# A two-layer decoder kernel: the routing stage of its mixture of experts worked in batch pairs, and seven of sixteen pairs of the shared expert moved to the combine stage

## The chip, the core and the metric

The kernel runs on one core of a Trainium2 chip. A core has a matmul engine (TensorE, PE in the rows; PEld is its weight load), VectorE (DVE), ScalarE (ACT), GpSimd (POOL) and SyncE (SP, which here only issues DMAs). They run side by side and wait for each other through semaphores. The metric is the device time of one launch in microseconds (us). The kernel before took 4232.36 us, the median of three runs (4230.83 to 4232.46).

## The reference, cut to what matters

The input x has B = 32 batches of S = 100 rows of D = 256 floats. Six blocks are added to it one after another: causal attention, a cross attention, an attention block with a small mixture of experts, a second attention, a wide cross attention, and last a mixture of NE = 8 experts with a shared expert beside them. Only that last block is touched by the change:

```python
def _L1_ffn_ref(x, shared_w1, shared_w2, experts_w1, experts_w2, gate_w):   # x: layer-normed rows
    x_flat = x.reshape(T, D)                                  # T = 3200 rows
    shared = jnp.einsum('td,dh->th', x_flat, shared_w1.T)     # 256 -> 1024
    shared = jnp.einsum('th,hd->td', jax.nn.silu(shared), shared_w2.T)   # 1024 -> 256
    gate_logits = x_flat @ gate_w.T
    top_k_gates, top_k_idx = jax.lax.top_k(gate_logits, TOP_K)            # 2 of 8
    top_k_gates = jax.nn.softmax(top_k_gates, axis=1)
    ...
    h = jnp.einsum('td,ehd->teh', x_flat, experts_w1)
    expert_out = jnp.einsum('teh,edh->ted', jax.nn.silu(h), experts_w2)
    selected = jnp.einsum('ted,te->td', expert_out, gates)
    return (shared + selected).reshape(B, S, D)
x = x + _L1_ffn_ref(_layernorm(x, axis=-1), ...)
```

## The kernel before, in words

Everything is float32, x stays in on-chip memory from the first stage to the last (`g.x`, 100 partitions by 32 batches by 256), and the stages run one after another, each a block with its own semaphores that all engines enter and leave together. The order inside a stage is written out by hand per engine: each engine has a `run(...)` that is called for every batch or tile, in a loop with a few calls unrolled at either end. In the trace a float32 matmul shows as two MATMULs with two weight loads.

The last block of the reference is three stages.

**Routing stage** (`route_phase`, L2423 to L2666). One batch at a time, 32 times. DVE takes the mean and variance (L80, L84), POOL the inverse root (L89, L91), DVE normalises (`route_y`, L96), PE transposes the 100x256 rows (L102), ACT copies them out of PSUM (`route_yT`, L2543). PE then does, in this order, the gate (L2497), the first layer of the shared expert (`shared_hidden`, L2505: 16 matmuls with a 128x128 block of `w_moe_shared` as weights and the 100 columns of one batch moving), two small matmuls that count the rows ahead of each row (`place`, L2512 and L2513), the second layer of the shared expert for the batch before (`shared_out`, L2520: 8 matmuls with the hidden rows as weights and 256 columns moving), and the transposes of the next batch. ACT applies silu to the hidden rows (L2549). DVE ranks the eight gates (`choose`, L2574 to L2578, with L855 to L865), turns ranks and counts into two slots per row (`place`, L2585 to L2602) and adds the shared expert's output to x (L2607). POOL scatters the normalised rows by these slots to a buffer in device memory (`slots`, L2472, two indirect DMAs per batch). At the end DVE works out the gates' softmax and, for the tiles of the next stage, which expert and which slots each has (L2627 to L2666). At the stage's start SP loads the shared expert's weights (L2457) and then the eight experts' weights, 16 times 1 MB (L2460).

**Tile stage** (`tiles_phase`). The scattered rows lie sorted by expert, in tiles of P = 128 rows; TILES = 58 tiles are worked whatever the routing. Per tile PE does 8 matmuls of 512 columns (L2743), transposes (L2752, L2734) and 8 matmuls of 256 columns in two layers of one expert (L2762).

**Combine stage** (`combine_phase`, L2806 to L2862). Per batch POOL gathers two rows per row back (L2826, two indirect DMAs, eight buffers), DVE multiplies them by the gates and adds them to x (L2835, L2837), SP stores the batch (L2858). PE and ACT do nothing here.

## Time and profile before

| | |
|---|---|
| time, median of three runs | 4232.36 us |
| profiled execution, its own time | 4235.83 us |
| its span in the trace | 4233.9 us |
| PE busy, whole span | 3860.0 us, 91% |
| DVE, ACT, POOL busy, whole span | 2055.6, 1657.3, 1428.3 us |
| routing stage | about 3360 to 3660 us |
| tile stage | about 3662 to 4134 us |
| combine stage | about 4137 us to the end |

The span is what the profiler saw between the first and the last instruction. A busy PE is not a PE at its peak: matmuls overlap, and the records' ends are modelled, so the pace of a run of matmuls is read from start to start. The granted clock (PEclk) is the share of TensorE's full speed that the chip allows; 1.00 is 2.4 GHz and 0.50 is 1.2 GHz.

### The profile page before, as it was taken

What the parts mean: (1) busy time and instruction counts of PE and PEld (TensorE: products, weight loads), DVE (VectorE), ACT (ScalarE), POOL (GpSimd) and SP (SyncE); (2) the same over time, 40 slices, a digit from 0 to 9 for tenths busy, and PEclk for the clock granted to TensorE, in tenths of its full rate; (3) what the DMA queues carried; (4) which work ended last, traced back from release to release, by engine and by line L of the source; (5) the groups of instructions that cost most, each with busy time, mean ns of one, the idle gap of its engine ahead of it and who ended that gap; (6) DMA issues with size and microseconds to landing.
All of it is one profiled execution on the core that took longest, in us unless ns stands there. A gap on an engine that the chain in (4) does not pass through costs nothing. (4 is left out here: it accounts for less than half of the span.)

```text
span 4233.9 us, 71248 instructions
## 1 busy us (share of the span) xinstructions
PE 3860.0 (91%) x25328; PEld 2484.8 (59%) x25329; DVE 2055.6 (49%) x6619; ACT 1657.3 (39%) x3559; POOL 1428.3 (34%) x1985
## 2 busy tenths in 40 slices
PE   6997899988999996888799999999999799899990
PEld 4775555555666653444366666666666588666770
DVE  3554666655777764343355455555555344321113
ACT  3553555554333322666344444444444211122220
POOL 0001433334444432011155555555555433100007
PEclk9999999998999998999899999999999799999995
DMA  9200111100000002000000000000000220011103
GB/s 293 112 0 23 46 34 41 37 1 1 1 0 0 1 1 51 1 1 0 11 12 6 7 12 6 6 12 7 6 12 1 99 105 24 26 34 33 32 30 96
DMA packets 80182, 129.31 MB, mean 31 GB/s; under 512 B 17099, under 2 KB 63600, under 8 KB 77296
## 3 DMA queue, kind: packets, MB, share of 16 engines
q1 hardware_dynamic: 71792, 113.28, 8.7%
q0 software_dynamic: 8192, 13.15, 1.1%
q8 instruction: 153, 2.51, 0.2%
q14 instruction: 45, 0.37, 0.0%
HBM read 78.00 MB, written 48.37 MB: 30 GB/s over the span
## 5 line engine op out<-in xcount | busy, mean ns | idle before, releaser
L2101 POOL TENSOR_SCALAR wide_probs<-wide_probs,wide_inverse 100x361 f32<-100x361 f32 x512 | 606.2, 1196 | 0.1
L2282 ACT ACTIVATE wide_probs<-wide_probs,wide_least 100x361 f32<-100x361 f32 x512 | 300.9, 589 | 629.1 <-DVE wide_least L2348 629.1
L2348 DVE CUSTOM_DVE_ANT_0 wide_probs<-banks,wide_bias 100x361 f32<-100x361 f32 x512 | 251.6, 529 | 124.8 <-issue 124.8
L399 PE MATMUL banks<-w_mix_expert,mix_m_x1T 128*100 128x512 f32 x512 | 258.9, 630 | 17.3 <-DVE mix_m_sum L757 15.8
L1822 ACT ACTIVATE rot_h<-banks,w_rot_b 128x800 f32<-128x800 f32 x256 | 223.6, 926 | 130.4 <-PE banks L1694 128.7
L2157 PE MATMUL banks<-w_wide_v,wide_c 64*120 64x512 f32 (+1 forms) x1152 | 263.5, 590 | 2.5 <-DVE wide_v L2334 1.8
L2151 PE MATMUL banks<-wide_c,w_wide_k 64*128 64x361 f32 x1536 | 255.4, 464 | 3.1 <-DVE wide_kT L2331 2.3
L2099 POOL TENSOR_TENSOR wide_hold_pool<-eps 100x1 f32<-100x1 f32 x256 | 50.7, 198 | 580.6 <-DVE wide_inverse L2354 579.1
L2193 PEld LDWEIGHTS banks<-ident,wide_probs 100*120 100x120 f32 (+1 forms) x1536 | 159.3, 172 | 148.3 <-issue 119.2
L2179 PE MATMUL banks<-wide_kT,wide_qT 64*100 64x361 f32 x1024 | 222.3, 511 | 1.7 <-issue 1.6
L2743 PE MATMUL banks<-moe_w,tiles_xT 128*128 x464 | 211.1, 598 | 0.6 <-DVE tiles_xT L2791 0.6
L2762 PE MATMUL banks<-moe_w,tiles_hT 128*128 x928 | 210.0, 380 | 1.0 <-DVE tiles_hT L2796 1.0
L2193 PE MATMUL banks<-ident,wide_probs 100*120 100x100 f32 (+1 forms) x1536 | 204.6, 270 | 6.8 <-POOL wide_probs L2101 6.8
L2354 DVE RECIPROCAL wide_inverse<-wide_rowsum 100x2 f32<-100x2 f32 x256 | 42.5, 166 | 341.6 <-ACT wide_probs L2282 341.6
L2151 PEld LDWEIGHTS banks<-wide_c,w_wide_k 64*128 64x128 f32 x1536 | 148.9, 187 | 91.9 <-ACT wide_kT L2273 4.5
L2210 PE MATMUL banks<-wide_probsT,wide_v 120*64 120x100 f32 (+1 forms) x3072 | 192.1, 260 | 0.5 <-DVE wide_headsT L2362 0.5
L2762 PEld LDWEIGHTS banks<-moe_w,tiles_hT 128*128 128x128 f32 x928 | 172.1, 190 | 22.4 <-issue 1.7
L757 DVE SCALAR_TENSOR_TENSOR mix_m_sum<-banks,mix_m_coef,mix_m_sum 100x256 f32<-100x256 f32 x256 | 123.6, 483 | 123.1 <-PE banks L399 114.3
L1012 POOL TENSOR_TENSOR cross_kroot<-cross_kclip,neg_half 121x8 f32<-121x8 f32 x64 | 104.2, 1638 | 227.2 <-DVE cross_kclip L1434 227.2
L2157 PEld LDWEIGHTS banks<-w_wide_v,wide_c 64*120 64x120 f32 (+1 forms) x1152 | 108.0, 181 | 120.4 <-issue 92.5
L2824 POOL TENSOR_TENSOR combine_hold<-eps 100x1 f32<-100x1 f32 x32 | 9.1, 285 | 488.6 <-DVE combine_slot_i L2831 487.8
L2210 PEld LDWEIGHTS banks<-wide_probsT,wide_v 120*64 120x64 f32 (+1 forms) x3072 | 141.5, 138 | 33.0 <-issue 1.5
(394 smaller groups left out, 7985.0 us busy)
## 6 DMA issues: line engine op xcount, KB each, us to landing
slots<-zeros SPq DMA_DIRECT2D x59, 512.0 KB, 5.7
moe_w<-in_moe_w SPq DMA_DIRECT2D x16, 1024.0 KB, 25.1
cross_c<-in_ctxT SPq DMA_DIRECT2D x32, 270.8 KB, 4.3
wide_c<-in_ctxT SPq DMA_DIRECT2D x32, 270.8 KB, 4.1
tiles_rows<-slots SPq DMA_DIRECT2D x58, 128.0 KB, 2.0
slots<-tiles_out SPq DMA_DIRECT2D x58, 128.0 KB, 1.7
cross_raw<-in_ctx SPq DMA_DIRECT2D x32, 180.0 KB
out<-x SPq DMA_DIRECT2D x32, 100.0 KB
```

The costliest lines, as they stand in the source:

```text
L399: last = nc.tensor.matmul(expert_bank[0:S, :], u.x1T[:, lane, c, :], w.expert[:, c, k * 2 * D:(k + 1) * 2 * D], start=(c == 0), stop=(c == ...
L1822: nc.scalar.activation(t.h[:, u % 2, m, 2 * half:2 * half + 2, :], pair_banks(i), ACT.Tanh, bias=w.b1[:, m:m + 1]).then_inc(h_done[i], 1)
L2101: last = nc.gpsimd.tensor_scalar(t.probs[:, i % RING, j, :], t.probs[:, i % RING, j, :], t.inverse[:, i % RING, j:j + 1], None, ALU.mult)
L2151: last = nc.tensor.matmul(make_bank(lane)[:, 0:CTX], w.k[rows_of(lane), k, at:at + P], t.c[rows_of(lane), of.buf, k, :], start=(k == 0), s ...
L2157: last = nc.tensor.matmul(make_bank(lane)[0:kw, :], t.c[rows_of(lane), of.buf, k, k0:k0 + kw], w.v[rows_of(lane), k, of.hf * BANK:(of.hf + ...
L2179: last = nc.tensor.matmul(scores(j), t.qT[rows_of(j), here.hf, m, lane, :], t.kT[rows_of(j), here.hf, m, lane, :], start=True, stop=True)
L2193: last = nc.tensor.transpose(turned(j)[0:kw, k * S:(k + 1) * S], t.probs[:, i % RING, j, k0:k0 + kw], g.ident[0:S, 0:S])
L2210: last = nc.tensor.matmul(heads_bank[rows_of(j), :], t.v[0:kw, of.hf, k, lane, at:at + WD], t.probsT[0:kw, i % RING, j, k * S:(k + 1) * S] ...
L2282: last = nc.scalar.activation(t.probs[:, i % RING, j, :], t.probs[:, i % RING, j, :], ACT.Exp, bias=t.least[:, i % RING, j:j + 1], scale=-1.0,
L2348: last = nc.vector.tensor_tensor_reduce(t.probs[:, i % RING, j, :], scores(j), t.bias[:, :], -1.0, LARGEST, ALU.add, ALU.min, t.least[:, i ...
L2743: last = nc.tensor.matmul(hid_bank(lane, half), t.xT[:, lane, c, :], f.w1[:, e, c, half * BANK:(half + 1) * BANK], start=(c == 0), stop=(c ...
L2762: last = nc.tensor.matmul(bank(7)[:, 0:D], t.hT[:, m, :], f.w2[:, e, m, :], start=(m == 0), stop=(m == HM - 1))
```

## The change

It has four parts, all in or for the last block.

1. **Pairs in the routing stage.** Each `run` now works a pair of batches: gates, ranks, counts and slots of both lanes in one instruction each, four scatters per pair, and the first shared layer with 200 columns moving. The rows `route_y` lie in four buffers (`ROW_RING`) where there were two. The running count of the second lane is made on DVE (`counted`) before `place` on PE.
2. **Where the shared expert is worked.** The routing stage does it for nine pairs: the eight even ones, spread over two `run`s each, and the last one after the loop. The seven other odd pairs (`LATER_PAIRS` = 1, 3, ..., 13) are done in the combine stage by PE, ACT and DVE, beside the gathers; mean and inverse root of all odd pairs are kept for that in `moe_meanvar` and `moe_rstd`. The store of these pairs waits for their sum.
3. **57 tiles** where there were 58; that is the most that 6400 rows over 8 experts can need.
4. **Loads and tail.** The shared expert's weights are loaded by SP during the wide cross attention stage, and stay until the end. The tables of the tiles are made ahead of the softmax of the gates, and both beside the last pair's matmuls.

```diff
@@ wide_cross_phase, SP
+            for sem, dst, src in g.loads:
+                sp.dma_start(dst, src).then_inc(sem, 16)
             with sp.Fori(1, PAIRS // 2) as two:
@@
-TILES = 2 * ROWS_ALL // P + NE
+TILES = (2 * ROWS_ALL + (NE - 1) * P) // P
+ROW_RING = 4
+HALF_HID = HM // 2
+LATER_PAIRS = list(range(1, PAIRS - 1, 2))
+SHARED_IN_ROUTE = PAIRS - len(LATER_PAIRS)
+def shared_hidden(nc, g, w, yT, half, ready):
+    for m in range(half * HALF_HID, (half + 1) * HALF_HID):
+        for c in range(DC):
+            last = nc.tensor.matmul(g.psum[:, m // 2, m % 2 * LANES * S:(m % 2 + 1) * LANES * S], w.shared1[:, c, m * P:(m + 1) * P], yT[:, c, :, :].rearrange("p l s -> p (l s)"),
+                                    start=(c == 0), stop=(c == DC - 1))
+    last.then_inc(ready, 1)
...
@@ route_phase, GpSimd
+            def scatter(of):
+                pool.wait_ge(s.slots, of.n)
+                nc.gpsimd.tensor_tensor(u.hold[:, of.buf:of.buf + 1], g.eps[0:S, :], g.eps[0:S, :], ALU.add)
+                for lane in range(LANES):
+                    for k in range(2):
+                        nc.gpsimd.indirect_dma_start(slots[:, :], bass.IndirectOffsetOnAxis(ap=slot_i[:, of.buf, lane, k:k + 1], axis=0), u.y[:, of.buf, lane, :],
+                                                     None).then_inc(scattered[of.buf], 16)
+            def run(before, here, after, third):
+                if third:
+                    roots(third)
+                scatter(here)
@@ route_phase, TensorE
+            def run(before, here, after, third):
+                even = here.par == 0
+                gate(here)
+                if even:
+                    hidden(here, 0)
+                else:
+                    shared_out(before, 0)
+                place(here)
                 if after:
                     turn_rows(after)
+                if even:
+                    hidden(here, 1)
+                else:
+                    shared_out(before, 1)
             turn_rows(FIRST)
-            batches(pe, run)
-            pe.wait_ge(s.added, B - 1)
-            shared_out(LAST)
-            pe.wait_ge(s.slots, B)
-            nc.tensor.matmul(bank(7)[0:S, 0:NE], w.all[:, :], u.running[:, 0, :], start=True, stop=True).then_inc(s.totals_ready, 1)
+            runs(pe, run)
+            pe.wait_ge(s.running, PAIRS + 1)
+            nc.tensor.matmul(totals_out, w.all[:, :], u.running[:, 0, 0, :], start=True, stop=True).then_inc(s.totals_ready, 1)
+            hidden(LAST, 0)
+            hidden(LAST, 1)
+            shared_out(LAST, 0)
+            shared_out(LAST, 1)
@@ route_phase, VectorE
-            dve.wait_ge(s.running, 1)
+            def apply(of):
+                if not of.fixed or of.pair >= ROW_RING:
+                    dve.wait_ge(scattered[of.buf], of.earlier_uses(2 * LANES * 16))
+                for lane in range(LANES):
+                    norm_apply(nc, dve, m1, lane, of.lane_n[lane], u.y[:, of.buf, lane, :], g.x[:, of.b[lane], :], s.y)
+                if of.par == 1:
+                    nc.vector.tensor_copy(f.meanvar[:, of.pair, :, :], m1.meanvar[:, :, :])
+                    nc.vector.tensor_copy(f.rstd[:, of.pair, :], m1.rstd[:, :, 0])
...
+            def run(before, here, after, third):
+                choose(here)
+                if after:
+                    apply(after)
+                if third:
+                    stats(third)
+                place(here)
+                if here.par == 1:
+                    add(before)
@@ combine_phase
+            turn_rows(0)
+            for j in range(LATER):
+                pe.wait_ge(s.yT, j + 1)
+                for half in range(2):
+                    shared_hidden(nc, g, w, t.yT, half, hid_ready[half])
+                if j < LATER - 1:
+                    turn_rows(j + 1)
+                shared_out(j)
...
             for k in range(GATHER):
-                add(k, B - GATHER + k, B - GATHER + k + 1, 32 * ROUNDS)
+                slots_of(k)
+            apply(0)
+            for b in range(B):
+                add(b)
+                j, step = b // PER_PAIR, b % PER_PAIR
+                if step == 0 and j + 1 < LATER:
+                    apply(j + 1)
+                if step == 1 and j > 0:
+                    add_shared(j - 1)
@@ combine_phase, SyncE
+                if b // LANES in LATER_PAIRS:
+                    sp.wait_ge(s.shared, LATER_PAIRS.index(b // LANES) + 1)
+                sp.dma_start(out[b], g.x[:, b, :]).then_inc(stored[b % GATHER], 16)
```

TensorE in the routing stage before, one batch of the loop: the gate, the first shared layer, the two count matmuls, the second shared layer of the batch before, the next batch's transposes (here `x2`, `x16` are repeats of one form; a name ahead of the arrow is written, the others are read).

```order
L2497 MATMUL banks<-w_moe_gate,route_yT 100x8 x2
L2505 MATMUL banks<-route_yT,w_moe_shared 128x100 x16
L2512 MATMUL banks<-route_mask,w_moe_earlier 100x8
L2513 MATMUL banks<-route_running,w_moe_all 100x8
L2520 MATMUL banks<-w_moe_shared,route_hidden 100x256 x8
L2491 REGISTER_ALU
L102 MATMUL banks<-ident,route_y 128x100 x2
```

TensorE there now, two pairs (four batches) of the loop, an even and an odd one:

```order
L2545 MATMUL banks<-w_moe_gate,route_yT 100x8 x4
L2437 MATMUL banks<-route_yT,w_moe_shared 128x200 x8
L2551 MATMUL banks<-route_mask,w_moe_earlier 100x16
L2552 MATMUL banks<-route_running,w_moe_all 100x16
L2538 ISA
L2447 MATMUL banks<-ident,route_y 128x100 x4
L2437 MATMUL banks<-route_yT,w_moe_shared 128x200 x8
...
L2563 MATMUL banks<-w_moe_shared,route_hidden 100x256 x8
L2551 MATMUL banks<-route_mask,w_moe_earlier 100x16
L2552 MATMUL banks<-route_running,w_moe_all 100x16
L2538 ISA
L2447 MATMUL banks<-ident,route_y 128x100 x4
L2563 MATMUL banks<-w_moe_shared,route_hidden 100x256 x8
```

The next pair's transposes stand between the two halves of the shared work, where they were the last thing before the next gate; four batches have one shared first layer of 200 columns where they had four of 100.

VectorE in the combine stage before, one batch of the loop:

```order
L2835 SCALAR_TENSOR_TENSOR x<-combine_got,moe_gate,x 100x256
L2836 REGISTER_ALU
L2837 ISA
L2837 SCALAR_TENSOR_TENSOR x<-combine_got,moe_gate,x 100x256
L2831 ISA
L2831 COPY combine_slot_i<-moe_slot_i 100x2
```

VectorE there now, batches 4 and 5 and the start of 6; `combine_y` are the rows for the shared expert and L2977 is its sum:

```order
L2964 SCALAR_TENSOR_TENSOR x<-combine_got,moe_gate,x 100x256
L2966 SCALAR_TENSOR_TENSOR x<-combine_got,moe_gate,x 100x256
L2951 COPY combine_slot_i<-moe_slot_i 100x2
L2958 TENSOR_SCALAR combine_y<-x,moe_meanvar,moe_rstd 100x256 x2
L2964 SCALAR_TENSOR_TENSOR x<-combine_got,moe_gate,x 100x256
L2966 SCALAR_TENSOR_TENSOR x<-combine_got,moe_gate,x 100x256
L2951 COPY combine_slot_i<-moe_slot_i 100x2
L2977 TENSOR_TENSOR x<-x,banks 100x512
L2964 SCALAR_TENSOR_TENSOR x<-combine_got,moe_gate,x 100x256
```

The sum of a shared pair, which waits for PE, stands in DVE's queue ahead of the rest of the gathered batches.

## Rows read from the trace of the kernel before

**Rows 1.** Busy time by stretch: length, then busy (instructions) per engine, PEclk, DMA.

```profile
3371.00:3392.70 21.70, 18.55 (x101) 17.15 (x101) 7.53 (x45) 4.09 (x8) 6.02 (x9) 0.71 1.02 423
3392.70:3641.00 248.30, 236.38 (x1682) 207.52 (x1682) 122.64 (x696) 38.58 (x87) 89.29 (x146) 1.00 0.14 50
3665.00:4133.00 468.00, 465.85 (x1971) 323.43 (x1970) 89.04 (x173) 103.24 (x174) 0.00 (x0) 0.99 0.10 32
4133.00:4234.00 101.00, 0.12 (x1) 0.00 (x0) 37.13 (x97) 0.00 (x0) 74.39 (x96) 0.52 0.35 99
```

**Rows 2.** Timeline, PE, one routing batch: start, length, engine, line, out<-in, count.

```profile
3606.83 0.52 PE L2497 MATMUL banks<-w_moe_gate,route_yT 128*100 128x8 f32 x4 [0.41 <-ACT route_yT L2543]
3607.20 3.79 PE L2505 MATMUL banks<-route_yT,w_moe_shared 128*128 128x100 f32 x32
3610.83 0.26 PE L2512 MATMUL banks<-route_mask,w_moe_earlier 100*100 100x8 f32 x2
3611.13 3.68 PE L2520 MATMUL banks<-w_moe_shared,route_hidden 128*100 128x256 f32 x16
3614.64 0.34 PE L102 MATMUL banks<-ident,route_y 100*128 100x100 f32 x2
3615.39 0.52 PE L2497 MATMUL banks<-w_moe_gate,route_yT 128*100 128x8 f32 x4 [0.41 <-ACT route_yT L2543]
```

**Rows 3.** Timeline, 200-column matmuls of the wide stage.

```profile
3119.78 2.02 PE L2144 MATMUL banks<-wide_yT,w_wide_q 128*128 128x200 f32 x11
```

**Rows 4.** Timeline, DVE and POOL, the same routing batch.

```profile
3607.38 0.17 DVE L2574 COPY route_gates<-banks 100x8 f32<-100x8 f32 x1
3608.76 0.17 DVE L2577 TENSOR_SCALAR route_mask<-route_rank 100x8 f32<-100x8 f32 x1
3611.38 0.17 DVE L2585 TENSOR_TENSOR route_running<-route_running,route_mask 100x8 f32<-100x8 f32 x1 [2.38 <-PE banks L2513]
3612.76 0.25 POOL L2470 TENSOR_TENSOR route_hold<-eps 100x1 f32<-100x1 f32 x1 [4.37 <-DVE route_slot_i L2596]
3613.07 0.17 DVE L2602 TENSOR_REDUCE route_logits<-route_picked 100x16 f32 x1
...
3614.55 0.98 POOL L2472 DMA_INDIRECT slots<-route_y,route_slot_i  x1 [0.30 <-issue]
```

**Rows 5.** DVE group of one line, 3392.7 to 3641: count, busy, mean ns, idle before.

```profile
L2607 DVE TENSOR_TENSOR x<-x,banks 100x256 f32 x29 | 12.2, 421 | 38.4 <-PE banks L2520 38.4
```

**Rows 6.** Timeline, start of the routing stage.

```profile
3360.82 0.10 POOL L2465 MEMSET route_running<- 100x8 f32 x1 [10.25 <-POOLq L2865]
3368.05 0.43 DVE L80 BATCH_NORM_STATS2 route_ln_stats<-x 100x6 f32<-100x256 f32 x1 [8.63 <-DMA w_moe_shared<-in_moe_shared]
3371.20 0.84 PE L2497 MATMUL banks<-w_moe_gate,route_yT 128*100 128x8 f32 x4 [0.41 <-ACT route_yT L2543]
```

**Rows 7.** Timeline, end of routing and start of tiles.

```profile
3649.58 3.70 PE L2520 MATMUL banks<-w_moe_shared,route_hidden 128*100 128x256 f32 x16 [0.52 <-DVE x L2607]
3659.73 0.17 DVE L2666 CAST moe_tile_expert<-route_tile_expert 1x58 int32<-1x58 f32 x1
3664.52 0.66 PE L2734 MATMUL banks<-ident,tiles_rows 128*128 128x128 f32 x2 [11.14 <-DMA tiles_rows<-slots]
3665.80 5.96 PE L2743 MATMUL banks<-moe_w,tiles_xT 128*128 x8 [0.61 <-DVE tiles_xT L2791]
```

**Rows 8.** Timeline, the same line in two tiles running.

```profile
4096.55 3.60 PE L2743 MATMUL banks<-moe_w,tiles_xT 128*128 x8
4104.53 3.60 PE L2743 MATMUL banks<-moe_w,tiles_xT 128*128 x8
```

**Rows 9.** Timeline, combine stage: its first copies, first and last sums.

```profile
4137.13 0.68 DVE L2831 COPY combine_slot_i<-moe_slot_i 100x2 int32<-100x2 int32 x8 [3.48 <-PEq L2865]
4142.67 0.48 DVE L2835 SCALAR_TENSOR_TENSOR x<-combine_got,moe_gate,x 100x256 f32 x1 [4.86 <-DMA combine_got<-slots,combine_slot_i]
4230.29 0.48 DVE L2835 SCALAR_TENSOR_TENSOR x<-combine_got,moe_gate,x 100x256 f32<-100x256 f32 x1 [1.63 <-DMA combine_got<-slots,combine_slot_i]
```

More of the change, by code:

```diff
@@ L2422, in route_phase, with turn_pair @@
+def turn_pair(nc, g, out, rows):
+    for lane in range(LANES):
+        for c in range(DC):
+            at = (c * LANES + lane) * S
+            last = nc.tensor.transpose(out[:, at:at + S], rows[:, lane, c * P:(c + 1) * P], g.ident[0:S, 0:S])
+    return last
 def route_phase(nc, g, w, f, slots, experts_in):
     with ExitStack() as ctx:
-        s = semaphores(nc, ctx, "route", "running y yT_ready yT gates_ready gates cmp ties behind rank mask chosen prefix_ready "
-                       "placed val sum slot slots picked logits larger below gexp gsum grec hid_ready0 hid_ready1 hid0 hid1 out_ready added totals_ready above tiles "
+        s = semaphores(nc, ctx, "route", "running y yT_ready yT gates_ready gates cmp ties behind rank mask chosen counted prefix_ready "
+                       "placed val sum slot slots equal picked logits larger below gexp gsum grec out_ready added totals_ready above tiles "
@@ L2486, in _ @@
             pe.wait_ge(g.loaded.moe, g.total.moe)
-            pe.wait_ge(s.running, 1)
-            def turn_rows(batch):
-                lane, b, n, pairs = batch
-                pe.wait_ge(s.y, n)
-                turn(nc, g, bank(4), u.y[:, lane, :], DC).then_inc(s.yT_ready, 1)
-            def gate(batch):
-                pe.wait_ge(s.yT, batch[2])
-                for c in range(DC):
-                    last = nc.tensor.matmul(bank(5)[0:S, 0:NE], u.yT[:, c, :], w.gate[:, c, :], start=(c == 0), stop=(c == DC - 1))
-                last.then_inc(s.gates_ready, 1)
@@ L2523, in run, with turn_rows, gate @@
-            def run(before, batch, after):
-                gate(batch)
-                shared_hidden(batch)
-                place(batch)
-                if before:
-                    shared_out(before)
+            def turn_rows(of):
+                pe.wait_ge(s.y, of.lane_n[LANES - 1])
+                turn_pair(nc, g, turned, u.y[:, of.buf, :, :]).then_inc(s.yT_ready, 1)
+            def gate(of):
+                pe.wait_ge(s.yT, of.n)
+                for lane in range(LANES):
+                    for c in range(DC):
+                        last = nc.tensor.matmul(gates_out[:, lane * NE:(lane + 1) * NE], u.yT[:, of.par, c, lane, :], w.gate[:, c, :], start=(c == 0), stop=(c == DC - 1))
+                last.then_inc(s.gates_ready, 1)
@@ new lines, in place, with hidden @@
+            def place(of):
+                pe.wait_ge(s.counted, of.n)
+                nc.tensor.matmul(prefix_out, w.earlier[:, :], u.mask[:, :, :].rearrange("s l e -> s (l e)"), start=True, stop=False)
+                nc.tensor.matmul(prefix_out, w.all[:, :], u.running[:, of.par, :, :].rearrange("s l e -> s (l e)"), start=False, stop=True).then_inc(s.prefix_ready, 1)
+            def hidden(of, half):
+                shared_hidden(nc, g, w, u.yT[:, of.par, :, :, :], half, hid_ready[half])
@@ new lines, in shared_out @@
+            def shared_out(of, lane):
+                if lane == 0 and not (of.fixed and of.pair == 0):
+                    pe.wait_ge(s.added, of.shared - 1 if of.fixed else pe.snap(of.shared - 1))
+                for m in range(HM):
+                    if lane == 0 and m % HALF_HID == 0:
+                        pe.wait_ge(hid[m // HALF_HID], of.shared)
+                    last = nc.tensor.matmul(out_bank[:, lane * D:(lane + 1) * D], u.hidden[:, m, lane, :], w.shared2[:, m, :], start=(m == 0), stop=(m == HM - 1))
+                if lane == LANES - 1:
+                    last.then_inc(s.out_ready, 1)
@@ L2554, in _ @@
             keep_rows(FIRST)
-            batches(act, run)
+            runs(act, run)
+            silu(LAST, 0)
+            silu(LAST, 1)
             act.wait_ge(s.below, 1)
@@ L2617, in run, with add @@
+            def add(of):
+                dve.wait_ge(s.out_ready, of.shared)
+                nc.vector.tensor_tensor(x_pairs[:, of.pair, :], x_pairs[:, of.pair, :], out_bank, ALU.add).then_inc(s.added, 1)
+            def run(before, here, after, third):
+                choose(here)
+                if after:
                     apply(after)
-                if before:
+                if third:
+                    stats(third)
+                place(here)
+                if here.par == 1:
```

337 lines of the change are left out of this document (185 added, 152 removed).

## The prediction

> **What bounds the kernel now.** I read the page first (PE busy 91% of the span), then the busy time by stretch, then the timelines of the three stages that the change touches. The stretches say where PE sets the pace. In the running part of the routing stage PE is busy 236.38 of 248.30 us at a granted clock of 1.00, in the tile stage 465.85 of 468.00 us, and in the combine stage not at all, where POOL is busy 74.39 of 101 us [rows 1]. So two of the stages are PE's, and the third is paced by POOL's gathers, with PE free beside it.
>
> In the routing loop a batch takes 8.56 us from gate to gate (3606.83 to 3615.39) [rows 2]. From start to start: gate 0.37, first shared layer 3.63, counts 0.30, second shared layer 3.51, transposes and what follows 0.75. Of this last part two transposes need about 0.36 (0.34 is the record of both), and some 0.4 is the wait of the next gate for ACT's copy [rows 2].
>
> **What a matmul costs, by shape.** The first shared layer is 32 records of 100 columns at 3.63/32 = 113 ns. Two hundred columns moving against one 128x128 weight load take, in the wide stage, (2.02 - 0.33)/10 = 169 ns from start to start; the 0.33 is my estimate of the last record's own length, in proportion to its columns from the second layer, where 16 records of 219 ns spacing span 3.68, so that the last is 0.39 [rows 2, 3]. A pair's first layer was 64 records, 7.26 us; it becomes 32, 5.41 us. The second layer is the same work, 32 records of 219 ns = 7.02 us a pair [rows 2]. A shared pair is 12.43 us of PE.
>
> **The routing stage after.** Two pairs (an even and an odd run) hold one shared pair: four gates 1.48, two counts 0.60 (the 16 columns in place of 8 I price at nothing, since each record is far above its columns' time), eight transposes 1.44, one shared pair 12.43: 15.95 us, where four batches took 34.25. I add 0.15 per run for hand-overs, so 16.25. Eight such: 130.0. The last pair's shared work after the loop: 12.4. Sum at full clock 142.4.
>
> Is PE still the slowest? DVE: from gate to mask it takes 1.55 us, its placing 1.86 us (3611.38 to 3613.24) [rows 4]. With both lanes in one instruction the small ones grow little: I take 2.2 us for choosing (with the new add to the running count), 2.2 for placing, 0.8 for applying, 1.3 for statistics, 0.7 for the sum in every other run. About 7 us a pair against PE's mean of 8.1. Its bound from above is two batches of today without merging, 2 x 122.64/29 = 8.46 us [rows 1]. POOL: a batch's hold and two scatters take 2.77 us (3612.76 to 3615.53) [rows 4], a pair's some 5.7, and 89.29/29 = 3.08 busy per batch with the roots [rows 1], which with the gaps between scatters is about 7.5 us a pair. It fits under 8.1, with little to spare. The wait inside a run is covered as well: PE's count waits for 2.2 us of choosing and has half a first layer (2.7) or a lane of the second (3.5) ahead of it; the copy of the transposed rows now has the other half ahead of the next gate, so the 0.4 us wait per batch goes. The new wait of `apply` on the scatters is for rows four pairs back, over 20 us earlier. Behind it on DVE stand the placing and the sums, and POOL would wait for these; I price it at nothing.
>
> **Its first batches.** They cost more today: 21.5 us for the first two (3371.20 to 3392.7), 4.4 more than two in the loop, at a mean granted clock of 0.71 [rows 1, 6], PE having idled since the wide stage. The price for the new stage lies between nothing and about 11 (all of the 21.7 us at half clock). The nearest row is the start of the tile stage, where the first tile's first layer took 5.96 against 3.60 [rows 7, 8] and some 3.2 us were lost in all; I take 5, because the first runs also wait through a longer start. The Trainium skill ("TensorE: Matmul & The Clock Gate", Part 1) says that the throttled state is the default and that activity releases it. The routing stage's start bears this out only slowly: with PE busy 18.55 of 21.70 us the clock was still 0.71 in the mean. By the page alone the fuller queue would lose no more than the tile stage does, and the sum would be about 2 us lower.
>
> Gate to the end of the last shared matmul: 142.4 + 5 = 147.4. It was 3371.20 to 3653.28 = 282.1 [rows 6, 7]. **-134.7 us.**
>
> **Ahead of the first gate.** DVE began at 3368.05, after the shared weights had landed, while POOL was in the stage at 3360.82; the gate came 3.15 us after DVE [rows 6]. Now the weights are there. DVE starts at about 3361, and takes two batches through statistics, roots (0.84 each on POOL) and transposes at half clock: about 5.3 us, gate at 3366.3. **-4.9.** The moved loads stand in SP's queue behind the context of the first two pairs of the wide stage and ahead of the third's, which is needed tens of us later; that covers their 2 MB. The experts' 16 MB still have to be in by the tile stage: the DMA engines are full until 3392.7 and then for at most 0.14 x 248 = 35 us more [rows 1], some 67 us in all from the stage's start, and the new stage is over 150 long.
>
> **Behind the last shared matmul.** Today 11.24 us pass until the tile stage's first transposes: 6.6 of softmax and tables on DVE, 4.6 of stage change [rows 7]. Now the tables stand beside the last pair's 12.4 us on PE, and only one sum of 512 columns is left, 0.8 with its hand-over (421 ns for 256 columns [rows 5]). **-5.8.** The cover would be gone only if DVE's 7 us of tables began over 5 us late.
>
> **One tile less.** Tiles follow each other at 7.98 us (4096.55 to 4104.53) [rows 8]. **-8.0.**
>
> **The combine stage.** Before, the first add is at 4142.67 and the 32nd at 4230.29: 2.83 us a batch, POOL's pace; the last add ends about 4231.3 [rows 9]. After: PE has seven shared pairs, 7 x 12.43 + six transposes of pairs at 0.7 = 91.2 us. It can start after the slot copies (0.68), the first pair's rows (0.75), transposes at half clock and their copy: 4140.6. With 3.2 lost to the clock, as at the start of the tiles, it ends at 4235.0, and the sum of pair 13 stands in DVE's queue ahead of batches 30 and 31: 0.7 + 2 x 1.05. End of the adds 4237.8. **+6.5.** So PE takes over the pace here from POOL, by little: DVE waits for PE once per pair, and eight gather buffers (22 us of POOL) stand between. The stores of the last six batches go out together in 3 us; a store's own landing is unchanged, and I price this at nothing, with 1 us as the bound.
>
> **Sum.** -134.7 - 4.9 - 5.8 - 8.0 + 6.5 = -146.9. From the profiled execution's own 4235.83 us that is 4088.9; the median of the runs is 3.5 lower, so 4085.5. **I forecast 4086 us.**
>
> **Rivals.**
> 1. *The hand-overs set the routing pace* (DVE and POOL as calculated are at 7 and 7.5 us of 8.1). For: today 0.4 us a batch is lost between transposes and gate [rows 2], and DVE's upper bound of 8.46 is above PE's mean. Against: the order on PE puts half a layer ahead of each wait. If each run loses 1.0 instead of 0.15, 16 x 0.85 = 13.6 more: 4100. At DVE's bound plus the wait for the shared sum, 9 us a pair, 4101.
> 2. *The clock is kept through the stage changes*, which are shorter (5 us of idle PE, not 11), and the combine stage is close to POOL's pace: 5 + 3.2 + 3.2 less: 4075. Against: 0.71 and 0.52 in the rows of all such stretches [rows 1].
> 3. *PE stays at half clock in the combine stage*: 12.43 becomes about 24.5, so 7 x 12 + 4 = 88 more: 4174. For: the granted clock there is 0.52 today [rows 1]; against: PE idles there, and the tiles reach 3.60 us after one slow tile.
> 4. *Slower than before*: the granted clock is low through both stages, because the new mix of short waits and long runs never fills PE. The 142 + 91 us of PE work would need 233 x (1/c - 1) more, and the gain of 147 is gone at a mean clock c of 0.61; at 0.50 the time is 4319. Against: 1.00 at 95% busy in today's loop [rows 1].
> 5. *The change doesn't shorten the routing stage's loads*: if the third pair's context in the wide stage waited for the 2 MB, that stage grows by at most 5 us: 4091.
>
> **Chances.** The forecast 57%, rival 1 20%, rival 2 11%, rival 5 4%, rival 3 5%, rival 4 2%, and 1% for no change. The forecast's own range is 4078 to 4096. The range for 8 in 10 reaches over rivals 1, 2 and 5 and not to 3 and 4: 4070 to 4114; the upper end takes in hand-overs of 1 us together with the longest slow start. A difference under 0.2% (8.5 us) can't be told from no change here. Faster 0.97, same 0.01, slower 0.02.
>
> **What would show it.** In the profile after: gates of even pairs about 16.2 us apart, PE over 95% busy at 1.00 between them; the 200-column shared matmuls at 169 ns; first gate 5 to 6 us after the last wide sum; a gap of about 5.5 us between the last shared matmul and the first tile; 57 tiles at 7.98; in the combine stage DVE waiting for PE about six times, PE busy 90 us. Wrong would be: POOL without idle time in routing, DVE's count later than PE's half layer, or a granted clock near 0.5 in a stage where PE is busy.

## The result, and the profile after

The changed kernel took 4061.6 us (median of four runs, 4055.7 to 4068.1), the kernel before 4231.6: ratio 0.960, 95% interval 0.958 to 0.962. The forecast was 4086, its range began at 4070; the gain is 170 us where 146 were forecast. The profiled execution took 4068.11 us, the slowest of the four, and stands against 4235.83 before.

| Stretch (us, profile to profile) | before | after | change | forecast |
|---|---|---|---|---|
| start to the end of the last VectorE operation of the wide stage | 3359.42 | 3354.94 | -4.5 | 0 |
| to the first gate | 11.77 | 6.27 | -5.5 | -4.9 |
| first gate to end of last shared product | 282.08 | 136.14 | -145.9 | -134.7 |
| to the first tile's transposes | 11.24 | 5.17 | -6.1 | -5.8 |
| tiles | 468.60 | 461.05 | -7.6 | -8.0 |
| stage change | 4.01 | 3.93 | -0.1 | 0 |
| combine, first slot copy to last sum | 94.16 | 95.50 | +1.3 | +6.5 |
| to the end | 2.58 | 3.29 | +0.7 | 0 |

The stretches of the changed stages, busy time and instructions for PE, weight loads, DVE, ACT and POOL, then granted clock and DMA, answer to [rows 1]:

```profile
3361.20:3378.60 17.40, 17.39 (x96) 15.87 (x97) 10.27 (x56) 3.80 (x5) 9.48 (x19) 0.87 1.01 419
3378.60:3476.70 98.10, 98.10 (x625) 88.60 (x624) 69.88 (x367) 16.62 (x26) 72.27 (x114) 1.00 0.39 142
3502.50:3963.60 461.10, 458.87 (x1938) 317.91 (x1938) 87.49 (x170) 101.49 (x171) 0.00 (x0) 0.99 0.10 32
3967.50:4063.00 95.50, 90.98 (x476) 79.36 (x476) 44.51 (x117) 14.51 (x21) 73.74 (x96) 0.97 0.35 100
```

The first row's mean clock of 0.87 is one stretch at half clock, then full clock to the end; before, there were two. The stretches at half clock, two from the kernel before (inside the first of [rows 1]) and then the one of the changed kernel:

```profile
3371.20:3376.80 5.60, 5.60 (x27) 5.60 (x28) 1.44 (x8) 1.75 (x2) 0.32 (x1) 0.50 1.01 427
3380.20:3387.10 6.90, 6.24 (x29) 5.94 (x30) 2.14 (x12) 0.83 (x2) 3.04 (x4) 0.51 1.01 413
3361.20:3365.80 4.60, 4.59 (x18) 4.60 (x19) 2.85 (x14) 1.25 (x1) 0.86 (x3) 0.50 1.01 424
```

Before, the clock was full between 3376.80 and 3380.20, where PE had 1.51 us of work (it waited 2.13 us for the second batch's rows), and then fell again. Now no wait of PE stands there, and the clock does not fall again.

In the stretch 3378.60:3476.70 PE is busy for all of the 98.10 us at full clock: no hand-over costs anything. PE's timeline of one even and one odd run answers to [rows 2]; it has no wait in brackets on any row:

```profile
3408.99 0.79 PE L2545 MATMUL banks<-w_moe_gate,route_yT 128*100 128x8 f32 x8
3409.64 2.95 PE L2437 MATMUL banks<-route_yT,w_moe_shared 128*128 128x200 f32 x16
3412.43 0.27 PE L2551 MATMUL banks<-route_mask,w_moe_earlier 100*100 100x16 f32 x2
3412.54 0.33 PE L2552 MATMUL banks<-route_running,w_moe_all 100*100 100x16 f32 x2
3412.78 0.56 PE L2447 MATMUL banks<-ident,route_y 100*128 100x100 f32 x4
3413.18 2.90 PE L2437 MATMUL banks<-route_yT,w_moe_shared 128*128 128x200 f32 x16
3415.91 0.79 PE L2545 MATMUL banks<-w_moe_gate,route_yT 128*100 128x8 f32 x8
3416.56 3.68 PE L2563 MATMUL banks<-w_moe_shared,route_hidden 128*100 128x256 f32 x16
...
3424.20 0.79 PE L2545 MATMUL banks<-w_moe_gate,route_yT 128*100 128x8 f32 x8
```

Read from start to start: gates 0.65, half a first layer 2.79 and 2.73, counts 0.35, four transposes 0.40; the two runs take 15.21 us (3408.99 to 3424.20).

The start of routing, [rows 6], and its end, [rows 7]:

```profile
3356.38 0.75 DVE L80 BATCH_NORM_STATS2 route_ln_stats<-x 100x6 f32<-100x256 f32 x2 [1.44 <-PEq L3003]
3361.21 1.00 PE L2545 MATMUL banks<-w_moe_gate,route_yT 128*100 128x8 f32 x5 [0.58 <-ACT route_yT L2595]
...
3490.33 0.17 DVE L2734 CAST moe_tile_expert<-route_tile_expert 1x57 int32<-1x57 f32 x1
3497.39 0.69 DVE L2682 TENSOR_TENSOR x<-x,banks 100x512 f32<-100x512 f32 x1 [3.61 <-PE banks L2563]
3502.52 0.66 PE L2810 MATMUL banks<-ident,tiles_rows 128*128 128x128 f32 x2 [5.17 <-DMA tiles_rows<-slots]
```

VectorE now starts behind the stage change, not behind the weights. The tables are done 7 us before the last shared product; only the sum at 3497.39 and the stage change are left. Two tiles running are 7.98 us apart as in [rows 8].

The combine stage, [rows 9]: one pair on PE, and what VectorE waited for in all of it (total, times, longest):

```profile
4035.30 5.58 PE L2437 MATMUL banks<-combine_yT,w_moe_shared 128*128 128x200 f32 x32
4040.71 0.51 PE L2447 MATMUL banks<-ident,combine_y 100*128 100x100 f32 x4
4041.05 7.07 PE L2921 MATMUL banks<-w_moe_shared,combine_hidden 128*100 128x256 f32 x32
4047.96 5.58 PE L2437 MATMUL banks<-combine_yT,w_moe_shared 128*128 128x200 f32 x32
```

```profile
DVE x L2964 <- DMA combine_got<-slots,combine_slot_i: 34.2, 24, 4.8
DVE x L2977 <- PE banks L2921: 12.7, 4, 5.1
```

PE takes 12.66 us a pair (4035.30 to 4047.96), so seven take 88.6, and VectorE waits for PE four times where I had said about six. The last shared sum waits 5.1 us for PE, and two batches' sums stand behind it, so PE's chain ends the stage; by how little, all_route and last_sum show below. A turn of four transposes costs 0.34 (4040.71 to 4041.05), where I had put 0.7.

### The profile page after: what moved, and what is told of

It is laid out like the page before. It is cut to its first block and busy times, and to the rows that moved or that the text cites. A ratio compares the mean times of both kernels' runs of the same rounds, so it can differ in the third digit from the quotient of the medians.

```text
span 4066.3 us, 69091 instructions
## 1 busy us (share of the span) xinstructions
PE 3810.0 (94%) x24746; PEld 2442.7 (60%) x24747; DVE 2014.0 (50%) x6326; ACT 1649.4 (41%) x3515; POOL 1419.9 (35%) x1969
```

## The experiments

The kernels ran in four series, each on another chip, with the kernel before at 4229.5 to 4233.1 us in all of them. Times of one kernel vary by more than most of the edits cost: the changed kernel's median was 4061.6, 4085.9, 4065.2 and 4071.9 us in its four sets of runs, and the runs of tail_late alone lie 17 us apart (what is known of the reasons is told below). So most verdicts are read from the stage that the edit touches, in one profiled execution each:

| kernel | ratio to before (95%) | first gate to last product | combine |
|---|---|---|---|
| after, first runs | 0.960 (0.958-0.962) | 136.14 | 95.50 |
| after again, series 1 | 0.966 (0.964-0.968) | 136.51 | 118.25 |
| all_route, series 1 | 0.983 (0.982-0.985) | 225.67 | 93.46 |
| turn_twice, series 1 | 0.968 (0.966-0.970) | 142.69 | 122.71 |
| turn_last, series 1 | 0.970 (0.968-0.972) | 152.11 | 123.88 |
| after_b, series 2 | 0.961 (0.959-0.963) | 136.46 | 95.62 |
| one_gather, series 2 | 0.961 (0.958-0.964) | 136.46 | 95.61 |
| last_sum, series 2 | 0.960 (0.958-0.962) | 135.97 | 95.49 |
| loads_back, series 2 | 0.963 (0.961-0.965) | 136.28 | 95.55 |
| ring2, series 3 | 0.973 (0.971-0.975) | 184.92 | 95.61 |
| split_cols, series 3 | 0.968 (0.966-0.970) | 151.37 | 108.90 |
| pool_more, series 3 | 0.961 (0.959-0.963) | 136.13 | 97.08 |
| tail_late, series 3 | 0.963 (0.961-0.965) | 137.50 | 97.00 |
| after_c, series 4 | 0.962 (0.961-0.964) | 136.68 | 95.61 |
| keep_first, series 4 | 0.961 (0.959-0.963) | 136.53 | 94.67 |
| code_shift, series 4 | 0.963 (0.961-0.965) | 136.43 | 100.90 |

**The changed kernel again, three times.**

> The changed kernel once more, nothing edited. If the spread of its first four runs (4055.7 to 4068.1 us) is how this program varies, five more lie in the same band, with a median of 4058 to 4064, and a second profile has the routing stage (first gate to the last shared product) at 136.1 us within 0.5 while its span differs by some microseconds in stages that were not changed. Rival: the 4.5 us by which the last VectorE operation of the wide stage came earlier (3354.46 against 3358.94) belongs to the change; then the second profile has it at 3354.5 within 1 again. If it is chance, it lies anywhere between 3351 and 3360.

> The changed kernel a third time. Its first runs gave 4061.6 us with the combine stage at 95.5 us (first slot copy to last sum); the second series gave 4085.9 with 118.3, the other stages alike within 0.4 us, and with ScalarE and VectorE waiting up to 19.5 us on TensorE's results that its records show as long issued. If that belongs to the chip or the series on which it runs, this run shows one of the two levels again, 95 to 96 or 117 to 124 us, and nothing between; if it varies from run to run, the stage lies between them.

> The changed kernel a fourth time, beside the two others of this series. Two levels have been seen in the combine stage, 95.5 to 97 us (two series) and 118.3 (one series). Again one of the two; which of them tells how often the slow one comes.

Medians 4085.9, 4065.2 and 4071.9, where I had expected 4058 to 4064. The routing stage repeats within 0.6 us. Two things do not. First, the last wide operation ended at 3349.65, 3345.45 and 3363.42 us: the 4.5 us are within what chance does (it does more than the 3351 to 3360 that I had allowed), and the rival falls. Second, the combine stage took 118.25 in series 1 and 95.5 to 95.6 in the others; I call these its long and its short level. Series 1, timeline of PE, ACT and DVE in that stage:

```profile
4013.28 5.58 PE L2437 MATMUL banks<-combine_yT,w_moe_shared 128*128 128x200 f32 x32
4026.88 0.84 ACT L2944 ACTIVATE combine_hidden<-banks 128x800 f32<-128x800 f32 x1 [19.53 <-remote]
4027.86 3.70 PE L2921 MATMUL banks<-w_moe_shared,combine_hidden 128*100 128x256 f32 x8 [7.82 <-ACT combine_hidden L2944]
4032.61 0.84 ACT L2944 ACTIVATE combine_hidden<-banks 128x800 f32<-128x800 f32 x1 [4.89 <-remote]
4034.74 0.74 DVE L2958 TENSOR_SCALAR combine_y<-x,moe_meanvar,moe_rstd 100x256 f32<-100x256 f32 x2 [12.00 <-remote]
```

By its records PE had half of the first layer at 4016.1; ScalarE, which had been free since 4007.35, got it at 4026.88. The releaser "remote" is none that the trace shows; such a wait stands in no other series. The stretch began some 25 us into the stage and ended at 4034.7; after it each pair took 12.7 again. Inside it ScalarE got the two halves of a first layer 5.73 us apart (4026.88 and 4032.61); after it, 2.70 apart. So PE's results came at less than half of their pace while its records show the usual one. turn_twice and turn_last, in the same series, have it too (longest 20.3 and 28.5 us); all_route, without PE work there, has not. What makes TensorE's results late stays open.

**All pairs in the routing stage (all_route).** This edit and those below are shortened.

```
-LATER_PAIRS = list(range(1, PAIRS - 1, 2))
+LATER_PAIRS = []
 def run(before, here, after, third):   # TensorE
     gate(here); hidden(here, 0); place(here); turn_rows(after)
-    even: hidden(here, 1)    odd: shared_out(before, 0 and 1)
+    hidden(here, 1); shared_out(here, 0); shared_out(here, 1)
```

> All sixteen pairs' shared expert in the routing stage, in the pair-wise form with four row buffers; none in the combine stage. Theory one (TensorE paces the routing stage, and the combine stage goes at the gathers' pace with or without the shared expert): seven more pairs of 5.52 + 6.97 = 12.49 us, +87.4, and the combine stage back from 95.5 to the 94.2 of the kernel before, so 4061.6 + 87.4 - 1.3 = 4148 us. Theory two (the combine stage still pays for its seven pairs; bare of them it ends with GpSimd's 90.4 us of gathers): 4143. Theory three (working in pairs gives nothing by itself, all the gain is the move of seven pairs): 4231.6 less the 5 ahead of the first gate, 6 behind the stage and 8 of the tile, about 4212.

Against after_again of its series the routing stage is 89.2 us longer (theory one: 87.4; a pair is 13.8 to 14.2 us from gate to gate in the loop). The combine stage is 93.46, so at the short level the seven pairs cost it 2.1. The median of 4162.4 misses theory one's 4148 by 14 us. Its profiled execution, the fastest of the four, took 4152.8, and 3.1 us of the 4.8 over 4148 lie between the last shared product and the first tile (8.26 us for 5.17), which I had not foreseen and no run explains; of the slower three there is no profile. Theory three falls: in the routing stage, working in pairs alone is worth 282.1 - 225.7 = 56.4 us, the move 89.

**Transposes issued twice (turn_twice).**

```
+    turn_pair(nc, g, turned, u.y[:, of.buf, :, :])
     turn_pair(nc, g, turned, u.y[:, of.buf, :, :]).then_inc(s.yT_ready, 1)
```

> Every pair's four transposes in the routing stage are issued twice into the same place. Theory one (TensorE paces, and a transpose costs it what the changed trace shows, 0.37 to 0.40 us for four): +16 x 0.39 = +6.2, 4067.8 us. Rival one (the 0.18 us apiece of the prediction, the trace's span being only overlap): +16 x 0.72 = +11.5, 4073. Rival two (something else paces the stage and TensorE has room): 4061.6.

The stage grew by 6.18 us, 0.097 for each of the 64 added transposes: theory one. The median of 4099.6 is 32 above the 4067.8 expected; 27 of these are the long level of the combine stage (122.7 for 95.5).

**Transposes at the end of a run (turn_last).**

```
 place(here)
-turn_rows(after)
 hidden(here, 1) or shared_out(before, 1)
+turn_rows(after)
 # ScalarE: in even runs the copy of the rows now stands behind both silus
```

> In the routing stage the next pair's transposes are issued at the end of a run instead of ahead of its last half, so that nothing of TensorE's work stands between them and the next gates; ScalarE's copy (0.49 us) with the semaphores on both sides lies bare. Theory one (the hand-overs cost nothing in the changed kernel because 2.7 to 3.5 us of other work stand between each product and its use): each of 15 runs now waits 0.6 to 0.85 us, +9 to +13, 4071 to 4075 us. Rival one (a hand-over costs 0.15 us wherever it stands, as the prediction had it): +2.4 at most, 4064. Rival two (GpSimd's issue of the scatters paces the stage): under +3.

+15.6 us, 1.04 for each of 15 runs, above even theory one. PE's timeline:

```profile
3410.75 0.51 PE L2447 MATMUL banks<-ident,route_y 100*128 100x100 f32 x4
3412.22 0.87 PE L2545 MATMUL banks<-w_moe_gate,route_yT 128*100 128x8 f32 x8 [0.97 <-ACT route_yT L2595]
...
3420.27 0.51 PE L2447 MATMUL banks<-ident,route_y 100*128 100x100 f32 x4
3421.36 0.87 PE L2545 MATMUL banks<-w_moe_gate,route_yT 128*100 128x8 f32 x8 [0.58 <-ACT route_yT L2595]
```

From start to start the turn with its wait takes 1.47 us in an even run and 1.09 in an odd one, against 0.40 in a full queue; the gates behind the wait take 0.73 against 0.65. Two things make this more than expected. With the wait (0.97 and 0.58) taken off, the turn still takes 0.5, the length of its whole record, since nothing follows to cover its end. And in even runs ScalarE's copy stands behind the second silu, which the edit moved ahead of it: it starts 0.93 us after the turn, in odd runs 0.55.

**One gather a batch (one_gather), the last sums in another order (last_sum), the first rows kept (keep_first).**

```
-for j in range(2): indirect_dma_start(t.got[:, k, j, :], ...)     # one_gather
+for j in range(1): indirect_dma_start(t.got[:, k, j, :], ...)
-    if step == 1 and j > 0: add_shared(j - 1)                     # last_sum, keep_first
+    if step == 1 and 0 < j < LATER: add_shared(j - 1)
+add_shared(LATER - 1)                                             # behind the last batch
+    nc.scalar.copy(f.yT, turned)                                  # keep_first, in routing
-    shared_hidden(..., t.yT, ...)
+    shared_hidden(..., t.yT if j else f.yT, ...)
```

> Combine stage with one gather a batch instead of two (the second expert's row is replaced by the first's, its rows are left out); shared expert as in the changed kernel. Theory one (the late results of TensorE come from GpSimd's stream of gathers beside it): the stage is TensorE's 93 us and no wait over 2 us on a result already issued; about 4061 if the series is a slow one. Theory two (they come with the chip or series whatever the gathers do): the stage stays at 115 to 120 us, 4080 to 4086. In a fast series both give 4059 to 4062.

> In the combine stage the first pair's rows are made ahead of seven of the eight slot copies, the last shared sum comes behind the last two batches' sums, and their two outputs are stored last. TensorE starts 1.2 us earlier and the last sums no longer stand behind TensorE: -2 to -3 us against the changed kernel of this series if the stage ends on TensorE's chain; within 1 us if the last gather or the last store sets the end.

> In the combine stage TensorE starts at once: the transposed rows of the first later pair are kept from the routing stage (one more ScalarE copy of 0.49 us there), its rows and transposes are left out of the combine stage, the last shared sum comes behind the last two batches' sums and its outputs are stored last. Theory one (TensorE's chain ends the stage): TensorE starts 2.9 us earlier and has one turn of 0.35 less, so its last product lands 3 us earlier and GpSimd's gathers (last issued 90.4 us into the stage, sums about 2.7 after) take over: 95.5 down to 93 to 93.5, -2 to -3 us in all. Rival (the first product is later held up by half clock, which the idle time before it sets): no more than -1.

one_gather leaves out the second expert's rows; it measures time alone. Half of the gathers changes nothing (95.61): at the short level PE's chain ends the stage. What they do at the long level wasn't seen. last_sum moved the end by 0.6 us with the way to the end (95.49 + 3.10 against 95.62 + 3.53), its median by 2.0, which can't be told from none. By its own rule (within 1 us) the gathers then set the end, and its trace says so: the sums of the last two batches wait 2.51 and 1.53 us for them. So PE's chain is the last by under 1 us there. keep_first let PE start with the stage:

```profile
3965.32 8.63 PE L2437 MATMUL banks<-moe_yT,w_moe_shared 128*128 128x200 f32 x32 [3.96 <-PEq L3007]
...
4058.39 0.48 DVE L2966 SCALAR_TENSOR_TENSOR x<-combine_got,moe_gate,x 100x256 f32<-100x256 f32 x1 [1.59 <-DMA combine_got<-slots,combine_slot_i]
4059.31 0.68 DVE L2979 TENSOR_TENSOR x<-x,banks 100x512 f32<-100x512 f32 x1
```

The first layer takes 8.63 us, 1.5 more than in the first profile (7.14) and 3.1 more than 5.52, and the sums of the last batch wait for its gather. The stage is 0.95 us shorter than after_c's (1.3 with the way to the end), where 2 to 3 were expected. That is the rival's "no more than -1", and half clock does hold the first layer up, but the last gather takes over as theory one has it, so the run doesn't decide between them. No median shows any of these as better than the changed kernel.

**Loads in the routing stage again (loads_back).**

```
-for sem, dst, src in g.loads: sp.dma_start(dst, src).then_inc(sem, 16)   # wide stage
+for sem, dst, src in g.loads: sp.dma_start(dst, src).then_inc(sem, 16)   # routing stage
```

> The loads of the gate and shared weights stand again at the start of the routing stage instead of in the wide stage. Theory one (as in the prediction: the wait of 4.9 to 5.5 us comes back, and the longer idle time costs TensorE's clock at the start a little more): +5 to +8 us against the changed kernel of this series. Rival (the loads in the wide stage cost it what they save, so that nothing changes): within 1 us, with the wide stage 5 us shorter than its 1283.

Wide end to first gate 13.51 us against 6.27, +7.2, and the wait is the one of [rows 6]:

```profile
3361.32 0.75 DVE L80 BATCH_NORM_STATS2 route_ln_stats<-x 100x6 f32<-100x256 f32 x2 [8.68 <-DMA w_moe_shared<-in_moe_shared]
```

Nothing is added behind it: the routing stage is 136.28 even after twice the idle time, and the clock is at half for 4.9 us behind the first gate (5.3 in after_b). The rival falls.

**Two row buffers (ring2).**

```
-ROW_RING = 4
+ROW_RING = 2
```

> Two row buffers in the routing stage in place of four, all else as changed. Theory one (four buffers matter: with two, the rows of a pair wait until the scatter of the pair two before has landed, GpSimd issuing 5.3 us for a pair and the landing 2.7 more, which is later than the 3 us at which they are made now): a chain of 14.5 to 17 us for two runs in place of 15.2, so 0 to +15 us from first gate to last shared product (136.1 to 136.5 now), with VectorE shown waiting for the scatters. Rival (the buffers hide nothing, TensorE paces anyway): within 1 us.

+48.5 us, three times theory one's upper end. Timeline of one run, 10.46 us from the rows of one pair to those of the next (line 96):

```profile
3408.01 0.73 DVE L96 TENSOR_SCALAR route_y<-x,route_ln_meanvar,route_ln_rstd 100x256 f32 x2 [1.35 <-DMA slots<-route_y,route_slot_i]
3408.66 0.75 DVE L80 BATCH_NORM_STATS2 route_ln_stats<-x 100x6 f32 x2
3409.72 0.19 POOL L89 TENSOR_TENSOR route_ln_vareps<-route_ln_meanvar,eps 100x1 f32<-100x1 f32 x1 [3.64 <-DVE route_ln_meanvar L84]
3411.31 0.19 POOL L2516 TENSOR_TENSOR route_hold<-eps 100x1 f32 x1
...
3415.78 0.99 POOL L2519 DMA_INDIRECT slots<-route_y,route_slot_i  x1 [0.30 <-issue]
3418.47 0.74 DVE L96 TENSOR_SCALAR route_y<-x,route_ln_meanvar,route_ln_rstd 100x256 f32 x2 [2.72 <-DMA slots<-route_y,route_slot_i]
```

The rows wait for a scatter (2.7 us of landing), the statistics stand behind the rows on DVE, the roots behind the statistics, and the next scatter behind the roots on POOL: a circle of every run, where I had seen one of every other. The stretch from 3380 to 3510:

```profile
3380.00:3510.00 130.00, 101.74 (x568) 90.37 (x569) 65.03 (x342) 15.95 (x24) 66.81 (x107) 0.91 0.29 105
```

PE is busy 78% of it and the granted clock is 0.91 in the mean, so besides the waits some of PE's work ran at half clock.

**First layer lane by lane (split_cols).**

```
-matmul(out of 200 columns, w.shared1[:, c, m], yT[:, c, both lanes])
+for lane: matmul(out of 100 columns, w.shared1[:, c, m], yT[:, c, lane, :])
```

> The shared first layer as 64 products of 100 columns a pair (each lane by itself, each weight tile loaded twice) in place of 32 of 200, in both stages. Theory one (the gain of the pair form is the shared weight load: 113 ns a product as in the kernel before against 87 x 2 = 174): +1.74 us for each of 9 pairs in the routing stage, 136.3 + 15.7 = 152 us, and +12.2 in the combine stage, 107.8; together +28 us, 4090. Rival (only columns count, 85 ns for 100 of them): no change in either stage, 4062.

+15.0 and +13.3 us, against 136.4 and 95.6 of the changed kernel: theory one in both stages. In the combine stage the start at half clock was again the longer one (told under pool_more); against pool_more's 97.08 the edit cost 11.8, where 12.2 were expected. Half a first layer now takes 3.64 us from start to start (2.79 before the edit), the 32 records of [rows 2] over again:

```profile
3413.36 3.79 PE L2439 MATMUL banks<-route_yT,w_moe_shared 128*128 128x100 f32 x32
3417.00 0.27 PE L2553 MATMUL banks<-route_mask,w_moe_earlier 100*100 100x16 f32 x2
```

**More work for GpSimd (pool_more).**

```
+for k in range(1, 5): nc.gpsimd.tensor_tensor(u.hold[:, k * ROW_RING + of.buf], g.eps, g.eps, ALU.add)
```

> Four more small GpSimd operations ahead of each pair's scatters in the routing stage, some 1.2 us a pair. Theory one (GpSimd is close behind TensorE there: 7.0 to 7.4 us of work and issue in a mean run of 7.6): the stage takes GpSimd's pace of 8.2 to 8.6 us a run, 136.3 + 9 to 16 us. Rival one (GpSimd has the room because four row buffers let the scatters fall behind): under +2. In both VectorE's rows wait longer for the roots or for the scatters, which the waits would show.

No change; theory one falls. Between 3380 and 3470, first after and then pool_more:

```profile
3380.00:3470.00 90.00, 90.00 (x569) 80.55 (x568) 63.80 (x339) 15.40 (x24) 67.09 (x108) 1.00 0.39 144
```

```profile
3380.00:3470.00 90.00, 90.00 (x571) 80.58 (x570) 63.36 (x333) 15.26 (x24) 73.46 (x153) 1.00 0.33 115
```

The 45 added operations cost 6.4 us busy, half of what I took; with 13.7 us of gaps between scatters POOL is at 87 of 90 us. It is nearly full, but it does not pace. The combine stage of this run and of tail_late took 97.0 instead of 95.6: the stretch at half clock at its start lasted some 3 us longer, and the first layer took 8.73 us here for 7.14.

**Tables behind the last sum (tail_late).**

```
+add(LAST)
 dve.wait_ge(s.logits, PAIRS)   # softmax, tables
-add(LAST)
```

> Tables and softmax of the routing stage stand again behind the last pair's sum on VectorE. Theory one (as in the prediction: 6.6 us of small VectorE operations come bare again): last shared product to first tile transposes 5.2 + 5.8 to 6.6 = 11 to 11.8 us, so +6. Rival (the stage change waits for something else, as the first rows' load): under +2.

Last product to first tile transposes 10.82 against 5.2 us, +5.6: theory one, a little under its range.

**More instructions ahead of the combine stage's products (code_shift).**

```
+for k in range(16): turn_pair(nc, g, g.psum[:, 5, 0:DC * LANES * S], t.y)
 # VectorE: the next pair's rows now wait for the first half of this pair's first layer
```

> 64 more transposes (128 more instructions of TensorE) at the start of the combine stage, into a bank that nobody reads. In a fast series: +5.6 to +7 us in the stage and nothing else. In a slow series: theory one (the slow stretch of TensorE of 256 instructions lies where its instructions are fetched): it comes half such a stretch, 128 instructions, later against the start of the shared products or earlier by as much; theory two (it hangs on the time since the gathers began): it begins 26 to 28 us after the first slot copy again.

Series 4 had the short level; +5.3 us in the stage, a little under the range. The first products start 6.7 us later, but the half-clock stretch at the stage's start now falls on the added transposes, and the first layer takes 5.60 us instead of 7.14. It says nothing on the stretch of late results.

## Why the prediction was wrong

What it said of who waits for whom held, except for the combine stage's long level; the time came out 24 us under the forecast, because several costs were put too high, the routing cycle first. 20.8 of these lie between the profiles:

- **The routing cycle** (-11.3 of 20.8; the step "eight transposes 1.44" and "I add 0.15 per run"). Two runs take 15.2 us, not 16.25. Transposes: 0.77, not 1.44. I took the length of a record (0.34 for two) for its cost, as if nothing followed it; in a full queue only the spacing counts, and turn_twice measures 0.097 each. Gates: 1.29, not 1.48; the 0.37 for one batch was from start to start, but behind a wait, and turn_last has such gates dearer too (0.73 for 0.65). Hand-overs: nothing, not 0.30; turn_last shows what they cost once nothing covers them. Counts and the first layer each took 0.1 more than I had put. Eight cycles: 8.4 us.
- **The start** (in the 11.3): two first runs cost 2.2 us over two in the loop, not 5. The trace of before had 4.4 there, with 0.71 of clock; now it is 0.87. I read the 0.71 as a clock that comes back slowly. It was two stretches at half clock with a full one between, where PE waited for rows, and that wait is gone. What is left is the 4.6 us at half clock behind the first gate, which cost about half of their length. The Trainium skill ("TensorE: Matmul & The Clock Gate", Part 1) says that activity releases the throttled state. This trace agrees (0.50 for the first 4.6 us of busy PE, 1.00 behind them), and the sum that I had set beside that rule, 2 us lower, was nearer.
- **The combine stage**: +1.3, not +6.5. Six turns of 0.34 for 0.7 give 2.1, the first layer loses 1.6 to the clock where I had 3.2, and PE starts it 2.9 us into the stage where I had 3.5; small terms make the rest. That the clock cost 1.6 and not 3.2 is partly luck: in pool_more it cost 3.2. All this is the short level; at the level of series 1 it is +24, which no step foresaw, and which by accident gives the forecast's 4086.
- **Stages not changed**: -4.5 us, which is luck as far as is known: the changed kernel gave 14.0 less than before's profile in after_b and 4.0 more in after_c, in step with the time at half clock (last section). Another 3.0: the profiled run is 6.5 us above its median, and I had subtracted 3.5. Without these 7.5 us the time would have been 4069, still just under the range.

Right in size: the way to the first gate (-5.5 for -4.9; loads_back), the tables (-6.1 for -5.8; tail_late), the tile (-7.6 for -8.0), the 169 ns of 200 columns (5.52 us for 5.41 a layer; split_cols), the second layer (6.97 for 7.02). Rival 5 is wrong: the wide stage took 1283 us in both. Rival 1 is wrong in this kernel; ring2 shows one way to it that the four buffers hold off, 49 us. Rival 2 came true in part: of its 11.4 us, 2.8 at the start of routing and 1.6 in the combine stage, and nothing at the tiles, whose first layer took 6.36 us for 5.96. Rivals 3 and 4 are wrong, with a clock of 1.00 in the running part of routing and 0.97 in the combine stage. The range's low end of 4070 was too near: it did not allow for several terms being too large at once, nor for the 18 us by which unchanged stages vary.

## What to carry to other kernels

Price a matmul or transpose in a queue that stays full by the distance between starts, read where no wait stands ahead of it, and not by the length of its record; for the transposes the two differed by 1.8 times here. Cut a mean clock into its stretches before you carry it over to another kernel: 0.71 was two of them, and the wait between them did not survive the change. Before a ring of buffers is shortened, write down the whole circle of waits through every in-order engine: here it closed over two more queues than the obvious one and cost 49 us. Read a stage in more than one series before its number is used: the combine stage with PE's work in it had two levels, 22.8 us apart.

## What was not expected

- The last wide operation ended between 3345.5 and 3363.4 us over the changed kernel and its variants, whose code ahead of it is the same (but for the loads of loads_back). The granted clock falls to its half in many short stretches of the stages ahead of it, at other places in each run. Up to that operation it stood at half for 164 us in after_b (ended 3345.45), 198 in the first profile (3354.94), 205 in the kernel before (3359.42) and 212 in after_c (3363.42). That fits most of the spread of the medians at the short level; no run tests it.
- Twice the idle time of PE ahead of the routing stage (loads_back) cost its first runs nothing more: the clock was already at half when the idle time of the changed kernel ended.
- The long level of the combine stage, +22.8 us, in one of five sets of runs, and there in all three kernels with PE work in that stage.
